# A transformer kernel of eight stages: z's convolution on the tensor engine in three chunks, rotated keys and queries by transfers in two, in another order

## The chip, the cores and the metric

The kernel runs on one core of a Trainium2 chip, in one launch. The core has five engines with a row of instructions each: PE (TensorE, matrix products into the eight banks of PSUM), DVE (VectorE), ACT (ScalarE), POOL (GpSimd) and SP (SyncE), which here issues the transfers. An engine takes its row strictly in order; engines wait for each other by semaphores. The metric is the device time of one execution in microseconds (us), median of several runs; less is better.

## The reference

Four layers, each an attention-like part and a feed-forward part, with a residual and a layer norm after each: eight stages, on 2048 tokens of width 128. The change touches two of them. Stage 0 is a state-space mixer:

```python
xz = jnp.einsum('bld,ed->ble', x, in_proj_w)
xs, zs = jnp.split(xz, 2, axis=-1)
xc = jax.nn.silu(_dwconv_same(jnp.swapaxes(xs, 1, 2), conv_x_w, conv_x_b))
zc = jax.nn.silu(_dwconv_same(jnp.swapaxes(zs, 1, 2), conv_z_w, conv_z_b))
# ... delta, B, C from xc; h = dA_t * h + dBu_t over 256 tokens, 64 x 16 states
y = jnp.concatenate([y, jnp.swapaxes(zc, 1, 2)], axis=-1)
return jnp.einsum('ble,de->bld', y, out_proj_w)
```

`_dwconv_same` is a convolution over four neighbouring tokens, each channel by itself. Stage 1 is an attention with 16 heads of width 8, of which 4 are plain and 4 are rotated by position, followed by a mixture of experts:

```python
k_rope = k_rope * cos + rotate_half(k_rope) * sin
q_rope = q_rope * cos + rotate_half(q_rope) * sin
kk = jnp.concatenate([k, k_rope], axis=-1)
qq = jnp.concatenate([q, q_rope], axis=-1)
```

`rotate_half` swaps the two halves of the four rotated dimensions; the signs are in the table of sines. Stages 2 to 7 are a linear attention, a feed-forward part with binarized weights, two more attentions and two more mixtures of experts.

## The kernel before

All data are fp32 and stay on the core. The tokens are cut into four chunks of 512 (two sequences of 256), and each chunk goes through the eight stages. Chunks 0 and 1 have a lane each; chunks 2 and 3 share the third: stages 0 to 3 of chunk 2, then of chunk 3, then stages 4 to 7 of both. Each lane has its part of one SBUF tile, `arena`; the weights lie in `W`, constants in `CF`, the residual in `X`, its transposition in `XT`.

A stage is a list of steps (`stage_steps`), each with parts on one engine after the other. `PARTS` says which: "P3.58 A.68" is a part of PE, then one of ACT, and the numbers are the planner's durations. The place of every part in its engine's row is written out in a table, `TURNS`, by step, stage and chunk; where a part may run on either of two engines (as "V.69|G1.28"), a minus sign chooses the second. `order_of_steps` sorts the parts by it and hands out PSUM banks. So the order of each engine's row is fixed by numbers.

The steps of which is spoken below:
- 0.n: layer norm and transposition (four 128x128 products on PE). 0.w: the four taps of the convolution times the projection's weights, on DVE.
- 0.in, number 0: projection and convolution of x, as four products of PE over shifted columns, then Silu on ACT. Number 1: the projection of z, one product; its convolution on DVE, a TENSOR_SCALAR (L1938) and three SCALAR_TENSOR_TENSOR (L1941); then Silu.
- 0.dt, 0.dr, 0.du, 0.bc: delta, its product with x, B and C. 0.wr and 0.rp: delta times x goes to HBM and comes back repeated over the states. 0.db: times B, on POOL (L2498). 0.da: delta repeated on PE, its exponential on ACT. 0.st: the scan over the tokens, on DVE (L2126), 16 per chunk. 0.hc: its state times C, on DVE (L1935) or POOL (L2502). 0.ac: the sum over states, on PE. 0.y to 0.e: output, residual, feed-forward and norms.
- 1.kq, number 0 for keys and 1 for queries: two products on PE, one with the weights and one with the weights of the swapped halves; DVE multiplies the first by cosines and the second by sines (L1935), POOL adds them (L2526). 1.km: keys masked by head, four copies. 1.sc, 1.ex, 1.nm, 1.tr, 1.pv: scores, exponential, normalization, transposition and product with the values.
- 3.p, numbers 0 and 1: stage 3's weights are binarized: a reduction (L2313) and other instructions of DVE, two of POOL and a transposition.
- 4.a, 4.g, 4.st, 4.l: weights of stage 4 multiplied ahead of time.
- The helpers: L1216 is every product of PE, L1220 every transposition, L1668 every ACT instruction, L1935 every TENSOR_TENSOR of DVE.

## Time and profile before

| | |
|---|---|
| runs | 1312.79, 1313.94 and 1316.95 us, median 1313.94 |
| profiled execution | 1316.18 us, its span 1314.2 us |
| mean granted clock of PE | 0.975 of full rate |
| PE busy | 1262.0 us, 96% |
| PE weight loads | 888.8 us, 68% (beside the products) |
| DVE busy | 927.8 us, 71% |
| ACT busy | 901.5 us, 69% |
| POOL busy | 777.6 us, 59% |
| transfers | 66.74 MB, 51 GB/s on average |

The span is the time from the first to the last instruction. Busy shares are averages over stages with different limits, so the profile is also read in stretches; a time in us below is counted from the span's start.
### The profile page before, as it was taken

What the parts mean: (1) busy time and instruction counts of PE and PEld (TensorE: products, weight loads), DVE (VectorE), ACT (ScalarE), POOL (GpSimd) and SP (SyncE); (2) the same over time, 40 slices, a digit from 0 to 9 for tenths busy, and PEclk for the clock granted to TensorE, in tenths of its full rate; (3) what the DMA queues carried; (4) which work ended last, traced back from release to release, by engine and by line L of the source; (5) the groups of instructions that cost most, each with busy time, mean ns of one, the idle gap of its engine ahead of it and who ended that gap; (6) DMA issues with size and microseconds to landing.
All of it is one profiled execution on the core that took longest, in us unless ns stands there. A gap on an engine that the chain in (4) does not pass through costs nothing.

```text
span 1314.2 us, 25939 instructions
## 1 busy us (share of the span) xinstructions
PE 1262.0 (96%) x8634; PEld 888.8 (68%) x8634; DVE 927.8 (71%) x3613; ACT 901.5 (69%) x2507; POOL 777.6 (59%) x853
## 2 busy tenths in 40 slices
PE   8799689999998999999999999999999999999997
PEld 4355356668744777777776777777788877776665
DVE  5979988867768788767656454787597678655254
ACT  6848899968574898766867666376778758765231
POOL 2989987668457867575655855356524524433434
PEclk9769989999998999999999999999999999999999
DMA  8753000110061000111000101101200011002430
GB/s 284 203 131 95 9 1 2 58 58 2 1 197 34 1 2 2 58 73 30 37 2 2 65 1 68 65 2 66 84 3 2 1 62 29 1 1 66 112 98 24
DMA packets 26373, 66.74 MB, mean 51 GB/s; under 512 B 2945, under 2 KB 7809, under 8 KB 25473
## 3 DMA queue, kind: packets, MB, share of 16 engines
q1 hardware_dynamic: 26240, 65.10, 16.4%
q8 instruction: 69, 1.13, 0.3%
q14 instruction: 64, 0.52, 0.1%
HBM read 61.74 MB, written 3.34 MB: 50 GB/s over the span
## 4 chain that ended last, share of the span: by engine, by line
PE 82%; DVE 9%; ACT 4%; POOL 2%; issue 2%; POOLq 0%; DVEq 0%; ACTq 0%
PE bank L1216 71%; PE bank L1220 11%; DVE arena L2126 2%; ACT arena L1668 2%; DVE arena L1935 2%; ACT L1668 1%; DVE stats L1949 1%; DVE arena L2192 1%; DVE stats L1938 1%; POOL arena L2566 1%; ACT bank L1668 1%; DVE arena L2190 1%; ACT X L1668 0%; POOL stats L2489 0%; DVE arena L2204 0%
## 5 line engine op out<-in xcount | busy, mean ns | idle before, releaser
L1668 ACT ACTIVATE arena<-arena 128x256 f32<-128x256 f32 (+4 forms) x804 | 355.6, 447 | 31.8 <-DVE arena L2192 15.0
L1668 ACT ACTIVATE arena<-bank 128x512 f32<-128x512 f32 (+3 forms) x354 | 190.9, 570 | 199.4 <-PE bank L1216 125.0
L1216 PE MATMUL bank<-XT,W 128*128 128x512 f32 (+1 forms) x720 | 287.5, 534 | 0.4 <-DVE arena L2204 0.3
L1216 PEld LDWEIGHTS bank<-W,arena 128*128 128x128 f32 x1888 | 230.2, 193 | 41.1 <-issue 35.7
L2513 POOL TENSOR_TENSOR arena<-arena 128x512 f32<-128x512 f32 (+2 forms) x108 | 171.3, 1600 | 137.5 <-DVE arena L1935 55.1
L1216 PE MATMUL bank<-W,arena 128*128 128x128 f32 (+1 forms) x1888 | 239.1, 277 | 1.1 <-POOL arena L2513 0.7
L1216 PE MATMUL bank<-arena 128*32 128x128 f32 (+8 forms) x2864 | 222.2, 335 | 6.9 <-DVE arena L2192 4.1
L2565 POOL TENSOR_TENSOR arena<-arena 128x256 f32<-128x256 f32 x192 | 118.6, 618 | 169.6 <-DVE arena L2198 169.1
L2566 POOL TENSOR_TENSOR arena<-arena 128x512 f32<-128x512 f32 x192 | 201.0, 1047 | 0.0
L1216 PEld LDWEIGHTS bank<-arena 128*32 128x32 f32 (+4 forms) x2864 | 147.0, 151 | 79.6 <-issue 52.8
L1220 PE MATMUL bank<-CF,arena 128*128 128x128 f32 x1312 | 181.7, 277 | 8.7 <-POOL arena L2566 5.3
L1216 PEld LDWEIGHTS bank<-XT,W 128*128 128x128 f32 x720 | 128.7, 192 | 84.5 <-issue 77.9
L1220 PEld LDWEIGHTS bank<-CF,arena 128*128 128x128 f32 x1312 | 150.2, 142 | 51.8 <-issue 38.9
L1216 PE MATMUL bank<-arena,W 128*128 128x512 f32 (+3 forms) x388 | 163.5, 663 | 15.3 <-DVE arena L2126 8.0
L1668 ACT ACTIVATION_READ_ACCUMULATOR arena<-arena 128x1 f32 x768 | 146.3, 190 | 0.0
L1668 ACT ACTIVATE arena<-bank,W 128x512 f32<-128x512 f32 (+1 forms) x180 | 103.0, 618 | 49.0 <-PE bank L1216 36.2
L2204 DVE COPY arena<-bank 128x512 f32<-128x512 f32 x147 | 98.1, 683 | 48.8 <-PE bank L1220 47.8
L1216 PEld LDWEIGHTS bank<-arena,W 128*128 128x128 f32 (+1 forms) x388 | 56.6, 200 | 85.3 <-issue 64.0
L1668 ACT ACT_TABLE_LOAD x82 | 105.2, 1283 | 11.2 <-DVE arena L1935 3.3
L1935 DVE TENSOR_TENSOR arena<-bank,arena 128x512 f32<-128x512 f32 x98 | 65.3, 684 | 67.3 <-PE bank L1216 57.4
L2192 DVE CUSTOM_DVE_ANT_0 arena<-bank,CB 128x256 f32<-128x256 f32 x256 | 107.3, 419 | 0.0
L2190 DVE CUSTOM_DVE_ANT_0 arena<-bank,CB 128x128 f32<-128x128 f32 x256 | 73.0, 285 | 30.9 <-PE bank L1216 29.2
(153 smaller groups left out, 1693.6 us busy)
## 6 DMA issues: line engine op xcount, KB each, us to landing
arena<-rws SPq DMA_DIRECT2D x44, 512.0 KB, 5.7
arena<-rep SPq DMA_DIRECT2D x62, 256.0 KB, 5.4
arena<-rws SPq DMA_DIRECT2D x8, 384.0 KB, 10.9
W<-w SPq DMA_DIRECT2D x1, 2692.0 KB, 9.1
...
```

The source lines that it names most:

```text
L1216: return e.matmul(o, lhsT, rhs, start=start, stop=stop, skip_group_check=True)
L1220: ins = e.transpose(bank[b.i][:, j * 128:j * 128 + s.shape[0]], s, cst("ident"))
L1668: return e.activation(o, a, func, **kw)
L1935: return e.tensor_tensor(o, a, b, op)
L1938: return e.tensor_scalar(o, a, s1_, s2_, op0, op1) if op1 is not None else e.tensor_scalar(o, a, s1_, None, op0)
L2126: e.tensor_tensor_scan(h, bank[a.i][:, :], h, 0.0, ALU.mult, ALU.add).then_inc(done[a.i], 1)
L2190: e.tensor_tensor_reduce(px[:, j * 384:j * 384 + 128], bank[b.i][:, 0:128], bias[:, 0:128], -1.0, 3.4e38, ALU.add, ALU.min, nm[:, 2 * j:2 ...
L2192: e.tensor_tensor_reduce(px[:, j * 384 + 128:(j + 1) * 384], bank[b.i][:, 128:384], bias[:, 128:384], -1.0, 3.4e38, ALU.add, ALU.min, nm[: ...
L2204: e.tensor_copy(third(s, c, n), bank[b.i][:, :]).then_inc(done[b.i], 1)
L2513: e.tensor_tensor(h, h, w, ALU.mult).then_inc(has["gw"], 1)
L2565: e.tensor_tensor(px[:, :, 0:128], px[:, :, 0:128], rec[:, :, 0:1].to_broadcast([128, 2, 128]), ALU.mult)
L2566: e.tensor_tensor(px[:, :, 128:384], px[:, :, 128:384], rec[:, :, 1:2].to_broadcast([128, 2, 256]), ALU.mult).then_inc(has["pn"], 1)
```

## The change

1. z's convolution. In chunks 0, 1 and 2 (all but `SHIFTED`) z is projected and convolved as x is, by four products of PE: step 0.in has a number 2, with the tap weights of z. The table of taps grows from 512 to 1024 columns, and 0.w with it. Chunk 3 keeps the old way.
2. The rotation. In chunks 1 and 3 (`MOVED`) 1.kq gives way to 1.rq: one product, copied to SBUF by ACT; SP moves the rows of the copy by eight small transfers to where the swapped half stands; DVE multiplies the moved copy by sines (in place, both operands in SBUF) and the bank by cosines; POOL adds. So that the swap is a shift of whole partitions, the 128 partitions of keys and queries are laid out by dimension within groups of four heads (`by_dim`), for all chunks; the scores are the same sums in another order.
3. The order. `TURNS` has other numbers throughout.

```diff
-    "0.in": ("P3.58 A.68", "P.87 V2.95 A.68"), "0.w": "V.6",
+    "0.in": ("P3.58 A.68", "P.87 V2.95 A.68", "P3.58 A.68"), "0.w": "V1.2",
+    "1.rq": "P.87 A.6 D2.6 V1.4 G1.27",
...
+MOVED = (1, 3)
+SHIFTED = (3,)
+def second_in(c):
+    return 1 if c in SHIFTED else 2
+def turned_by(c):
+    return "1.rq" if c in MOVED else "1.kq"
...
-        add("0.in", 1, ("0.bc", 0))
+        add("0.in", second_in(c), ("0.bc", 0), *([] if c in SHIFTED else [("0.w", 0, PREP)]))
...
-    ("0.n", 0, 0): (11, 13, 14, 18, 26), ("0.in", 0, 0): (29, 41, 93, 103, 117), ("0.dt", 0, 0): (44, 48, 55), ("0.dr", 0, 0):
```

On SP:

```diff
+                elif name == "1.rq":
+                    on.wait_ge(*after("kr", name, c, n))
+                    raw, to = s1(c, 3 + n), s1(c, 5 + n)
+                    for g in range(0, 128, 32):
+                        e.dma_start(to[g:g + 24, :], raw[g + 8:g + 32, :]).then_inc(d_kq[c][n], 16)
+                        e.dma_start(to[g + 24:g + 32, :], raw[g + 16:g + 24, :]).then_inc(d_kq[c][n], 16)
```

On PE:

```diff
-                    if n:
+                    if n == 1:
                         mm(ps[:, :], wt(0, "win")[:, 128:256], s0(c, 1)).then_inc(full[b.i], 1)
                         continue
...
-                        tap = wt(0, "tap")[:, k * 128:(k + 1) * 128]
+                        tap = wt(0, "tap")[:, k * 256 + 64 * n:k * 256 + 64 * n + 128]
...
+                elif name == "1.rq":
+                    b, ps = first(name, c, n)
...
+                    mm(ps[:, :], wt(1, "kq" if n else "kr"), s1(c, 1)).then_inc(full[b.i], 1)
```

On ACT:

```diff
+                        act(s0(c, 7 if n else 6), bank[b.i][:, :], ACT.Silu, bias=wt(0, "czb" if n else "cxb")).then_inc(done[b.i], 1)
...
+                elif name == "1.rq":
+                    b = u("b", name, c, n)
+                    on.wait_ge(*filled(b))
+                    act(s1(c, 3 + n), bank[b.i][:, :], ACT.Copy).then_inc(has["kr"], 1)
```

On DVE:

```diff
-                    tt(taps, taps, wt(0, "win")[:, 0:128].unsqueeze(1).to_broadcast([128, 4, 128]), ALU.mult).then_inc(has["taps"], 1)
+                    tt(taps, taps, wt(0, "win").unsqueeze(1).to_broadcast([128, 4, 256]), ALU.mult).then_inc(has["taps"], 1)
...
+                elif name == "1.rq":
...
+                    on.wait_ge(d_kq[c][n], 128)
+                    own(tt(tm, tm, sn, ALU.mult))
+                    tt(d, bank[b.i][:, :].rearrange("p (b l) -> p b l", b=2), cs, ALU.mult).then_inc(done[b.i], 1)
+                    on.wait_ge(*own.last())
```

On POOL:

```diff
+                elif name == "1.rq":
+                    d = s1(c, 3 + n)
+                    on.wait_ge(*emptied(u("b", name, c, n)))
+                    e.tensor_tensor(d, d, s1(c, 5 + n), ALU.add).then_inc(has["kq"], 1)
```

The layout of the partitions:

```diff
+def by_dim():
+    g, d, j = np.meshgrid(np.arange(4), np.arange(8), np.arange(4), indexing="ij")
+    return (32 * g + 8 * j + d).reshape(128)
```

How the rows move, at three places. The lines have other numbers after the change: L1216 becomes L1242, L1220 L1246, L1935 L1971, L1938 L1974, L1941 L1977, L2126 L2162. First, PE's row at the start, before: the convolution of x of chunk 2 (the third to fifth line), the transposition of chunk 0 (the first L1220), 0.dt of chunk 2, 0.bc of chunk 2 with a small product ahead, and the transposition of chunk 1.

```order
L1216 MATMUL bank<-arena,W 128x512
L1216 MATMUL bank<-arena,W 128x2x255 x2
L1216 MATMUL bank<-arena,W 128x2x254
L1216 MATMUL bank<-W 128x128
L1220 MATMUL bank<-CF,arena 128x128 x4
L1216 MATMUL bank<-arena,W 128x512
L1216 MATMUL bank<-W,CF 128x128
L1216 MATMUL bank<-arena,W 128x512 x2
L1220 MATMUL bank<-CF,arena 128x128 x4
L1216 MATMUL bank<-arena,W 128x512
L1216 MATMUL bank<-arena,W 128x2x255 x2
L1216 MATMUL bank<-arena,W 128x2x254
```

After:

```order
L1242 MATMUL bank<-arena,W 128x512
L1242 MATMUL bank<-arena,W 128x2x255 x2
L1242 MATMUL bank<-arena,W 128x2x254
L1246 MATMUL bank<-CF,arena 128x128 x8
L1242 MATMUL bank<-arena,W 128x512
L1242 MATMUL bank<-W,CF 128x128
L1242 MATMUL bank<-arena,W 128x512 x3
L1242 MATMUL bank<-arena,W 128x2x255 x2
L1242 MATMUL bank<-arena,W 128x2x254
L1242 MATMUL bank<-arena,W 128x512
L1242 MATMUL bank<-arena,W 128x2x255 x2
L1242 MATMUL bank<-arena,W 128x2x254
```

The transpositions of chunks 0 and 1 now stand together ahead of chunk 2's 0.dt, and behind the convolution of x of chunk 0 stands that of z of chunk 2.

Second, DVE's row at the first scans of chunk 2. Before, from the end of 0.du:

```order
L1935 TENSOR_TENSOR arena<-bank,arena 128x512
L1938 TENSOR_SCALAR arena<-bank,W 128x512
L1941 SCALAR_TENSOR_TENSOR arena<-bank,W,arena 128x2x255 x2
L1941 SCALAR_TENSOR_TENSOR arena<-bank,W,arena 128x2x254
L1935 TENSOR_TENSOR arena<-bank,arena 128x512
L2126 SCALAR_TENSOR_TENSOR arena<-bank,arena 128x512
```

After (the first row holds the end of 0.du and the input of the first scan):

```order
L1971 TENSOR_TENSOR arena<-bank,arena 128x512 x2
L2162 SCALAR_TENSOR_TENSOR arena<-bank,arena 128x512
L1971 TENSOR_TENSOR arena<-bank,arena 128x512
L2162 SCALAR_TENSOR_TENSOR arena<-bank,arena 128x512
L1974 TENSOR_SCALAR arena<-bank 128x512
```

The four instructions of z's convolution are gone from between; the second scan has moved ahead of chunk 0's 0.dt.

Third, DVE's row at the first rotations of stage 1 (`bank,CF` is a bank times cosines or sines). Before:

```order
L1935 TENSOR_TENSOR arena<-bank,CF 128x512 x2
L2126 SCALAR_TENSOR_TENSOR arena<-bank,arena 128x512
L2313 TENSOR_REDUCE pre<-W 128x4
L1938 TENSOR_SCALAR bw<-W 128x512
L1938 TENSOR_SCALAR pre<-pre 128x4
L1941 SCALAR_TENSOR_TENSOR bw<-W,bw 128x512
L1938 TENSOR_SCALAR bw<-bw,pre 128x128 x4
L1935 TENSOR_TENSOR arena<-bank,CF 128x512 x4
L2126 SCALAR_TENSOR_TENSOR arena<-bank,arena 128x512
```

After:

```order
L1971 TENSOR_TENSOR arena<-bank,CF 128x512 x2
L2162 SCALAR_TENSOR_TENSOR arena<-bank,arena 128x512
L1971 TENSOR_TENSOR arena<-arena,bank 128x512
L2162 SCALAR_TENSOR_TENSOR arena<-bank,arena 128x512
L1971 TENSOR_TENSOR arena<-arena,bank 128x512
L1971 TENSOR_TENSOR arena<-bank,CF 128x512 x4
L2162 SCALAR_TENSOR_TENSOR arena<-bank,arena 128x512
```

The five lines of 3.p are gone; two state products (0.hc) and a scan stand there. 3.p has moved behind the router of chunk 2, right ahead of chunk 1's first softmax.

## Rows read from the trace of the kernel before

**Rows 1.** The page: busy times, and the chain that ended last, by engine.

```profile
PE 1262.0 (96%) x8634; PEld 888.8 (68%) x8634; DVE 927.8 (71%) x3613; ACT 901.5 (69%) x2507; POOL 777.6 (59%) x853
...
PE 82%; DVE 9%; ACT 4%; POOL 2%; issue 2%; POOLq 0%; DVEq 0%; ACTq 0%
```

**Rows 2.** Busy time by stretch: length, busy (instructions) of each engine, clock, DMA.

```profile
0.00:225.00 225.00, 193.21 (x1256) 110.46 (x1257) 188.24 (x556) 175.65 (x433) 171.57 (x144) 0.88 0.36 106
...
30.00:54.00 24.00, 16.08 (x52) 5.37 (x50) 20.70 (x27) 21.67 (x30) 23.36 (x13) 0.79 0.72 186
...
92.00:118.00 26.00, 26.00 (x148) 14.53 (x147) 21.88 (x34) 18.87 (x28) 25.10 (x17) 1.00 0.55 142
...
118.00:153.00 35.00, 27.03 (x172) 15.13 (x170) 33.71 (x83) 27.26 (x61) 30.75 (x22) 1.00 0.13 38
...
153.00:225.00 72.00, 61.84 (x676) 43.36 (x677) 64.22 (x316) 68.63 (x259) 56.58 (x66) 0.93 0.01 2
...
225.00:345.00 120.00, 119.63 (x941) 84.26 (x940) 93.11 (x372) 94.63 (x266) 85.23 (x89) 1.00 0.10 32
...
345.00:420.00 75.00, 65.61 (x313) 38.16 (x312) 59.07 (x140) 45.44 (x71) 45.65 (x34) 0.95 0.36 101
...
420.00:1314.00 894.00, 883.54 (x6128) 655.89 (x6126) 587.33 (x2549) 585.77 (x1738) 475.13 (x586) 1.00 0.11 35
```

**Rows 3.** The same view, of the stretch at the lower clock.

```profile
54.00:82.00 28.00, 26.88 (x93) 12.66 (x94) 21.32 (x26) 16.09 (x23) 24.99 (x15) 0.51 0.54 150
```

**Rows 4.** PE's waits, first line: total, times, longest.

```profile
PE bank L1216 <- DVE arena L2126: 14.9, 9, 4.7
```

**Rows 5.** Timeline, PE at the start: start, duration, what, idle before.

```profile
9.50 3.58 PE L1216 MATMUL bank<-arena,W 128*128 128x512 f32 x8
...
13.49 0.66 PE L1220 MATMUL bank<-CF,arena 128*128 128x128 f32 x4
...
14.03 1.12 PE L1216 MATMUL bank<-arena,W 128*128 128x512 f32 x2
```

**Rows 6.** Timeline, DVE at the start; the weights' load, from the list of transfers.

```profile
7.51 0.69 DVE L1935 TENSOR_TENSOR W<-W 128x512 f32<-128x512 f32 x1
...
12.33 2.35 DVE L1938 TENSOR_SCALAR arena<-X,stats 128x128 f32<-128x128 f32 x8
...
24.28 0.75 DVE L1938 TENSOR_SCALAR arena<-bank,W 128x512 f32<-128x512 f32 x1 [1.23 <-PE bank L1216]
...
25.07 2.31 DVE L1941 SCALAR_TENSOR_TENSOR arena<-bank,W,arena 128x510 f32<-128x510 f32 x3
...
W<-w SPq DMA_DIRECT2D x1, 654.0 KB, 5.5
```

**Rows 7.** 0.hc: the line on POOL, and DVE's group of that shape.

```profile
L2502 POOL TENSOR_TENSOR arena<-arena x33: 1257/1271/1296, 29.8 to 155.2; 128x512 f32<-128x512 f32 x33
...
L1935 DVE TENSOR_TENSOR arena<-arena,bank 128x512 f32<-128x512 f32 x14 | 9.1, 668 | 0.0
```

**Rows 8.** Timeline at 3.p: DVE, then PE's wait, then POOL.

```profile
137.14 0.66 DVE L2313 TENSOR_REDUCE pre<-W 128x4 f32<-128x512 f32 x1
...
138.78 2.88 DVE L1938 TENSOR_SCALAR pre<-pre 128x4 f32<-128x4 f32 x1
...
143.46 2.47 DVE L1935 TENSOR_TENSOR arena<-bank,CF 128x512 f32<-128x512 f32 x4
...
144.88 1.52 PE L1216 MATMUL bank<-arena,W 128*128 128x512 f32 x3 [3.46 <-DVE arena L1935]
...
139.82 1.82 POOL L2548 MEMSET arena<- 128x2080 f32 x1
```

**Rows 9.** Small transfers of SP by line, and landing times of a 256 KB write.

```profile
L1172 SPq DMA_DIRECT2D rws<-arena x48: 269/290/345, 236.4 to 1265.6; - x48
...
L1159 SPq DMA_DIRECT2D rep<-arena x4: 320/332/432, 23.1 to 374.8; - x4
...
DMA to landing us min/median/max: 2.0/2.1/2.3
```

More of the change, by code:

```diff
@@ L286, in stage_steps @@
         add("1.vz", 0, ("1.r", 0))
-        add("1.kq", 0, ("1.n", 0), ("1.a", 0, PREP))
-        add("1.kq", 1, ("1.n", 0))
-        add("1.km", 0, ("1.kq", 0))
-        add("1.km", 1, ("1.kq", 0))
+        kq = turned_by(c)
+        add(kq, 0, ("1.n", 0), ("1.a", 0, PREP))
+        add(kq, 1, ("1.n", 0))
+        add("1.km", 0, (kq, 0))
+        add("1.km", 1, (kq, 0))
         add("1.v", 0, ("1.n", 0), ("1.a", 0, PREP), ("1.vz", 0))
-        attention(lambda u: [("1.kq", 1), ("1.km", 0), ("1.km", 1), ("1.v", 0)], lambda u: [])
+        attention(lambda u: [(kq, 1), ("1.km", 0), ("1.km", 1), ("1.v", 0)], lambda u: [])
         add("1.y", 0, *[("1.pv", u) for u in range(UNITS)])
@@ L360, in weight_steps @@
 def weight_steps():
-    loads = [("load", s, 0, [need for q in OVER[s] for c in range(NC) for need in ([("f", 0, c, q)] if q else [("0.in", 1, c, 0), ("0.dt", 0, c, 0)])]
+    loads = [("load", s, 0, [need for q in OVER[s] for c in range(NC) for need in ([("f", 0, c, q)] if q else [("0.in", second_in(c), c, 0), ("0.dt", 0, c, 0)])]
               + [("4.st", n, PREP, 0) for n in range(4) if s == 4]) for s in OVER]
@@ L820, in network @@
         d_wr = [sem(f"d_wr{c}") for c in range(NC)]
+        d_kq = {c: [sem(f"d_kq{c}_{n}") for n in range(2)] for c in MOVED}
         d_rp = [[sem(f"d_rp{lane}_{i}") for i in range(STATES // 2)] for lane in range(LANES)]
@@ L908, in decays0, with gated @@
             return uses["AB"[q % 2], "0.da", c, q - q % 2]
+        def gated(c):
+            return after("zc", "0.in", c, 1) if c in SHIFTED else emptied(u("b", "0.in", c, 2))
         def by_pe(c, q):
@@ L1140, in stage_over @@
                     else:
-                        on.wait_ge(*after("zc", "0.in", c, 1))
+                        on.wait_ge(*gated(c))
                         on.wait_ge(*filled(u("b", "0.dt", c)))
@@ L1323, in _ @@
                     on.wait_ge(*emptied(uses["Y", "0.ac", c, 0]))
-                    on.wait_ge(*after("zc", "0.in", c, 1))
+                    on.wait_ge(*gated(c))
                     for j in range(4):
@@ L1373, in _ @@
                     banks = [u(f"S{j}", name, c, n) for j in range(4)]
-                    on.wait_ge(*after("kq", "1.kq", c, 1))
+                    on.wait_ge(*after("kq", turned_by(c), c, 1))
                     on.wait_ge(*after("km_a", "1.km", c, 0))
@@ L1748, in _ @@
                         on.wait_ge(*filled(b))
-                        act(s0(c, 6), bank[b.i][:, :], ACT.Silu, bias=wt(0, "cxb")).then_inc(done[b.i], 1)
+                        act(s0(c, 7 if n else 6), bank[b.i][:, :], ACT.Silu, bias=wt(0, "czb" if n else "cxb")).then_inc(done[b.i], 1)
                 elif name == "0.bc":
@@ L1805, in _ @@
                 elif name == "1.km":
-                    on.wait_ge(*after("kq", "1.kq", c, 0))
+                    on.wait_ge(*after("kq", turned_by(c), c, 0))
                     for i in (n, n + 2):
@@ L2168, in _ @@
                 elif name == "1.km":
-                    on.wait_ge(*after("kq", "1.kq", c, 0))
+                    on.wait_ge(*after("kq", turned_by(c), c, 0))
                     for i in (n, n + 2):
@@ L2692, in constants @@
          "rows8": np.concatenate([(q[:, 0:32] == 8 * k + p % 8) for k in range(4)], 1).astype(np.float32),
-         "hm": (p // 8 % 4 == np.arange(4)[None, :]).astype(np.float32), "gm": (p % 32 < 8).astype(np.float32), "half": np.full((128, 1), np.float32(0.125))}
+         "hm": (p % 4 == np.arange(4)[None, :]).astype(np.float32), "gm": (p % 32 < 8).astype(np.float32), "half": np.full((128, 1), np.float32(0.125))}
     cf = np.concatenate([d[n] for n, _ in CONSTS], 1).astype(np.float32)
```

45 lines of the change are left out of this document (26 added, 19 removed), and 491 rows, old and new, of tables (EMITS, OPENS, PARTS, TURNS).

## The prediction

> **What bounds the kernel now.** I read the page first: PE is busy 96% of the span, DVE 71%, ACT 69%, POOL 59%, and the chain that ended last stands on PE for 82% of it [rows 1]. So PE work costs its own time wherever PE is full, and help for another engine pays only where PE waits. Where is that? The table by stretches tells [rows 2]: PE is busy 119.63 us of the 120 from 225 to 345, and 883.54 of the 894 after 420. Before 225 it is idle 225 - 193.21 = 31.8 us, and it loses more by its clock: the granted clock is at the lower of its levels (1.2 of 2.4 GHz) for nearly all of 54 to 82 [rows 3]. So the first 225 us are the one large place for a gain. From 345 to 420 it is busy 65.61 of 75; these 9.4 idle us lie in stage 0 of chunk 3, which the change leaves as it is.
>
> What holds PE there? The list of PE's waits has scans by DVE at its head, 14.9 us in 9 waits [rows 4]. But DVE isn't alone: between 30 and 54 POOL is busy 23.36 of 24, between 92 and 118 25.10 of 26, where PE is itself busy 26.00 of 26. After 153 ACT has 68.63 of 72 [rows 2]. DVE leads from 118 to 153: 33.71 of 35, PE 27.03. A microsecond taken from DVE is a microsecond gained only there and before the first scan.
>
> **z's convolution on PE, in chunks 0, 1 and 2.** Before, PE makes one product for z and DVE convolves it in four instructions. After, PE does the four shifted products that it does for x. A group of eight PE instructions (four products) took 3.58 us [rows 5], so one product is 0.89 and each chunk adds 2.7 us of PE, 8.1 in all. It frees DVE of 0.75 + 2.31 = 3.06 us per chunk [rows 6], 9.2 in all. ACT makes the same Silu, from another place.
> - Chunk 2. DVE's convolution begins at 24.28 and ends at 27.38, right ahead of the first scan's input [rows 6]: gain 3.06. The new products of PE stand where PE waits anyhow. But the start has two costs. The product over the taps doubles from 512 to 1024 columns, 0.69 to 1.38, and its load of 654 KB, landed 5.5 us after its issue, grows by 256 KB; in proportion that would be 2.2 us, of which I take 0.6, since some of the 5.5 is spent before data flow. The load of before had landed by 1.8 + 5.5 = 7.3, and DVE took it up at 7.51, so the product now ends at about 7.5 + 0.6 + 1.4 = 9.5, and the convolution of x, which began at 9.50, loses 0.2. Then PE's row: the transposition of chunk 1 now stands ahead of chunk 2's 0.dt. DVE's work for it was ready at 12.33 + 2.35 = 14.68; the longer product ahead of it takes what DVE had to spare there, so about 14.9, and the transposition takes 0.66: 0.dt starts at 15.6, not 14.03 [rows 5, 6]. That is 1.6 later, with the 0.2 in it. Sum: -3.1 + 1.6 = -1.5. Ends: -3.1 and +1.6, and 1.6 more if the load takes the whole 2.2.
> - Chunk 0. DVE is let off once more; PE's 2.7 us fit into what it is idle between 30 and 54, 24 - 16.08 = 7.9 [rows 2]. POOL is the engine that is full there, and the order moves 0.hc steps between the two: by counting them, DVE has 2 more in chunk 0, 2 more in chunk 1 and 1 fewer in chunk 2, so POOL is freed of 3 x 1.27 = 3.8 us and DVE gets 3 x 0.67 = 2.0 [rows 7]. I take -2.0 for the exchange, about half of what POOL gains, since PE at its lower clock holds both up between 54 and 92. Ends: -3.8 and +2.0.
> - Chunk 1. The row places its convolution around 100 us, where PE is full [rows 2]: +2.7. The ends are 0 and +5.4, at the lower clock.
>
> **3.p is moved.** The two binarizations of stage 3's weights are needed only by stage 3, and stood in DVE's row among the first rotations. The first took DVE from 137.14 to 143.46, 6.3 us, and PE waited 3.46 us for the rotation behind it [rows 8]. It now stands ahead of chunk 1's first softmax. I take -4.5, between that wait and the whole stretch; ends 0 and -6.3. The second has the same kinds of instruction and came after 153, where ACT is the busy one: I take -1.0, ends 0 and, at the first one's price, -6.3 [rows 2]. In the new place, from about 225, DVE is busy 93.11 of 120 us and PE full [rows 2]; the stretch stands before a softmax of chunk 1 alone. I take +1.0, ends 0 and +6.3.
>
> One instruction in [rows 8] deserves a look: a TENSOR_SCALAR on 128x4, the smallest work there, took 2.88 us. It ended at 141.66, with POOL's memset (139.82 + 1.82 = 141.64). The Trainium skill, "SBUF — State Buffer", section "Who interferes with whom", says why: VectorE in its two-port modes and GpSimd hold a shared port pair by turns, a whole instruction long, and also a VectorE instruction with two SBUF inputs contends with a GpSimd instruction that reads SBUF. The trace agrees for the first kind. The page speaks against the new rotation, whose product of two SBUF tiles is of the second kind: by the rule it could stand behind POOL as this one did, which the last rival below prices.
>
> **Rotated keys and queries by transfers (1.rq), chunks 1 and 3.** It drops one product per half, four in all: -0.89 x 4 = -3.5 us of PE, in stretches where PE is full [rows 2, 5]. ACT gains four copies, DVE has its two products of 0.67 as before, POOL its sum. What it adds is delay. A half passes: a copy on ACT, 0.6 by my estimate (a product's time of 0.67 on DVE [rows 7]), eight transfers issued by SP at 0.29 each 2.3, landing 2.1 after the last (2.0 to 2.3 for a write of 256 KB): 5.0 us where a second product of 0.89 stood, 4.1 later [rows 5, 9]. The second half of a chunk has the first one's eight issues ahead of it, 6.4 later. DVE takes its row in order, so if the transfers aren't there, it stands with softmaxes of other lanes behind it; a PSUM bank too is held through the transfer. The order places other work between: in chunk 1, counted by steps, the first product stands two steps behind the chunk's transposition in place of four, and DVE comes to it eight steps later than to the old rotation. I take 1.1 us per chunk, +2.2. Ends: 0, and all of 2 x 6.4 = 12.8.
>
> **The sum.** -1.5 - 2.0 + 2.7 - 4.5 - 1.0 + 1.0 - 3.5 + 2.2 = -6.6 us. The profiled execution took 1316.18 us (span 1314.2), the median of the runs is 1313.94, 2.2 below it; the change is taken from the median: 1307.3 us.
>
> **The rivals.**
> - The clock. More products before 54 us leave PE less idle, and the stretch at the lower level from there may shrink or go. PE was busy 26.88 of 28 there; at the higher rate it would need half, but POOL needs 24.99 of the 28, so that at most 3.0 us come free: 1304.3 [rows 3]. For it: PE is sparse, 16.08 of 24, just ahead of that stretch, and the change puts 2.7 us there. Against: the start is late by 1.6. The Trainium skill, "TensorE: Matmul & The Clock Gate", section "What's actually happening", says that the rate follows how busy PE has been; by that rule this rival would hold, and the trace agrees in so far as the long low stretch follows a sparse one.
> - Relief that reaches nobody. POOL holds 30 to 118 and ACT what follows 153 [rows 2]; then the gains at the start, of the exchange and of 3.p (1.5, 2.0, 4.5 and 1.0) fall away, and 2.7 + 1.0 - 3.5 + 2.2 = +2.4 is left: 1316.3. For it: the busy shares. Against: PE's wait of 3.46 us for DVE, right behind 3.p.
> - Late transfers, the slower case. Chunk 1 comes to its rotation when the two other lanes are at the end of their attention and DVE is busy about nine tenths; if DVE stands for the landing in both chunks, the whole 12.8 us are paid in place of 2.2: -6.6 + 10.6 = +4.0, 1317.9. The new product of two SBUF tiles may besides stand behind a POOL instruction of 1.27 us each time, as the TENSOR_SCALAR did behind the memset [rows 7, 8]: 4 x 1.27 = 5.1, and alone it would make 1312.4. It decides from the point where DVE waits at 1.rq for more than 2.2 + 6.6 = 8.8 us in all. Against it: one chunk has two other lanes beside it each time, and PE is full after 420.
> - The change does what it says in any case: the products and transfers are in the rows of the new order.
>
> **From cases to numbers.** About 0.3% of 1314, 3.9 us, is what a measurement of this kernel can tell from no change. Forecast 0.48, own range 1303.3 to 1311.3; clock 0.17; no relief 0.22; late transfers 0.13. Of the forecast 0.07 lies within 3.9 us, so faster is 0.41 + 0.17 = 0.58. Within: 0.07 of the forecast, 0.15 of "no relief", 0.03 of the late transfers, 0.25. Slower: 0.07 + 0.10 = 0.17. The range runs to 1298.5 below, since the start and 3.p may both give their full price beside the clock, and to 1318.5 above.
>
> **What would show it.** First scan of DVE before 27.5 us; 0.dt of chunk 2 at about 15.6; three PE groups of eight more before 120; the first scores of stage 1, which follow on the rotation that PE waited for at 144.88, some 5 us earlier; PE's idle time before 225 down from 31.8 by those 5 and the 8.1 us of new products, 13 in all; DVE's wait for the transfers under 3 us in all; busy PE +4.6 us at equal clock. The forecast is wrong if that first rotation reaches PE no earlier than 144, or if DVE waits at 1.rq for over 8 us, or if a new wait appears ahead of chunk 1's softmax.

## The result, and the profile after

The changed kernel takes 1337.54 us (median of 4 runs, 1332.68 to 1341.45), the kernel before beside it 1314.49 us. The ratio is 1.0165, 95% interval 1.0143 to 1.0187: slower by 23 us, where 6.6 us less was forecast. Its profiled execution took 1341.45 us, its span 1339.7 us. It is the longest of the four, which lie in two pairs, near 1333 and near 1341 us. One run of e1 below took 1622.14 us at a granted clock of 0.743, and is left out of e1's ratio.

The page after: busy times, the clock in 40 slices, and the chain that ended last, by engine and by line.

```profile
PE 1277.2 (95%) x8644; PEld 898.1 (67%) x8644; DVE 920.3 (69%) x3608; ACT 901.4 (67%) x2507; POOL 771.6 (58%) x849
...
PEclk9769999899998979999999999999999999999999
...
PE 78%; DVE 8%; ACT 5%; POOL 3%; issue 2%; SPq 2%; DMA 1%; POOLq 0%; DVEq 0%; ACTq 0%
PE bank L1242 68%; PE bank L1246 10%; ACT arena L1700 4%; DVE arena L2162 2%; DVE arena L1971 1%; POOL arena L2543 1%; SPq L1184 1%; DVE arena L2237 1%; DVE stats L1985 1%; POOL arena L2547 1%; DVE stats L1974 1%; ACT L1700 1%; SPq L1185 1%; DVE arena L2235 1%; ACT X L1700 1%
```

Against [rows 1]: PE's share of the chain fell from 82% to 78%, and two newcomers stand in it, "SPq" (SP issuing transfers) and "DMA". L1184 and L1185 are the two `dma_start` lines of `1.rq`. 3% of 1340 us are 40 us: small shares of a chain are no small change.

Busy time by stretch, as in [rows 2, 3], and the two places that will matter (225 to 250 and 464 to 493):

```profile
0.00:225.00 225.00, 197.28 (x1256) 111.58 (x1257) 171.87 (x531) 170.21 (x424) 160.97 (x137) 0.89 0.36 107
225.00:250.00 25.00, 18.27 (x132) 10.59 (x130) 16.32 (x70) 17.36 (x52) 12.78 (x14) 0.86 0.20 50
...
440.00:464.00 24.00, 23.43 (x142) 17.55 (x140) 18.68 (x76) 19.92 (x47) 16.54 (x21) 1.00 0.00 1
464.00:493.00 29.00, 20.99 (x119) 16.02 (x119) 15.91 (x64) 16.66 (x58) 14.89 (x18) 0.71 0.08 19
...
30.00:54.00 24.00, 20.26 (x51) 7.41 (x52) 17.27 (x22) 15.77 (x24) 17.25 (x11) 0.72 0.72 184
54.00:82.00 28.00, 21.80 (x84) 8.30 (x82) 20.54 (x25) 16.24 (x22) 28.00 (x17) 0.72 0.48 133
...
118.00:153.00 35.00, 34.24 (x180) 21.62 (x177) 30.66 (x65) 27.87 (x54) 30.88 (x22) 0.90 0.16 46
153.00:225.00 72.00, 60.55 (x702) 40.43 (x701) 65.68 (x333) 69.95 (x269) 55.40 (x66) 1.00 0.01 2
225.00:345.00 120.00, 113.06 (x892) 80.22 (x890) 93.63 (x366) 93.81 (x268) 87.22 (x90) 0.97 0.12 37
```

By the first 225 us little is lost: the same 1256 matmuls as in [rows 2], PE idle for 27.7 us in place of 31.8. The stretch from 225 on, where PE had been full, isn't full any more.

**Where the lag grows.** Shares don't tell when time was lost. Both programs run the same steps (the order's names), so I took for each step of PE its start after less its start before, and the median over the steps that began in a stretch of 20 us of the kernel before. The columns to the right are the experiments' profiled executions, told below; plus is later, in us.

| stretch of before | after | e1 no transfers | h1 also old order late | i4 h1 with transfers | e7 | b1 3.p alone | f2 z alone |
|---|---|---|---|---|---|---|---|
| 120 | 9.9 | 3.7 | 4.1 | 4.5 | 10.1 | -0.3 | 3.7 |
| 200 | 0.9 | -5.5 | -5.0 | -4.6 | 1.3 | -3.5 | 2.2 |
| 220 | 1.9 | -2.7 | -2.8 | -3.6 | 2.2 | -3.5 | 2.2 |
| 240 | 8.8 | -0.6 | -1.8 | 4.0 | 7.8 | -1.9 | 2.2 |
| 260 | 9.8 | 0.4 | -0.8 | 4.9 | 8.8 | 0.7 | 2.2 |
| 340 | 9.0 | -0.5 | -1.1 | 4.7 | 7.9 | 2.1 | 2.2 |
| 380 | 12.4 | 4.4 | 1.6 | 6.2 | 9.8 | 3.1 | 3.5 |
| 440 | 12.7 | 5.1 | 0.8 | 4.8 | 6.3 | 3.2 | 4.1 |
| 460 | 25.9 | 11.4 | 0.8 | 20.9 | 19.5 | 3.2 | 4.1 |
| 1240 | 24.9 | 10.5 | 0.7 | 20.8 | 18.4 | 3.1 | 4.0 |

The column "after" has two jumps: 7 us at 240 and 13 at 460. Nothing happens after 480. The 10 us of lag at 120 are nearly gone at 200, where ACT is the busy one. Single executions differ: b1 and i2, below, hold the same instructions in their first 130 us and are 4.3 us apart at 120 (-0.3 and -4.6). So a difference of 3 or 4 us in one column is not a finding; the jumps are. They stand in e2's execution too, 7.3 us at 240 and 13.2 at 460, in a program that differs from the changed kernel in z's convolution alone.

**The first jump.** The chain of waits from 225 to 255, by line, and its pieces (start, length, what):

```profile
by line: PE bank L1242 26.4%; SPq L1184 20.1%; SPq L1185 14.8%; issue 7.4%; DMA arena<-arena 6.5%; DVE arena L2237 4.6%; PE bank L1246 3.4%; ACT arena L1700 3.3%; DVE arena L2235 3.1%; DVE arena L1971 3.1%; DVE arena L2039 2.1%; PE bank L14
...
225.80 0.88 SPq L1184
...
232.19 0.75 SPq L1184
...
237.31 1.97 DMA arena<-arena
239.33 0.57 issue
239.91 0.68 DVE arena L1971
```

SP's sixteen issues for chunk 1's queries and keys stand end to end from 225.80 to 237.93, 12.1 us, 0.76 each with the gaps. The second half's eight begin only at 232.19. What DVE did meanwhile:

```profile
231.13 0.68 DVE L1971 TENSOR_TENSOR arena<-arena,X 128x512 f32<-128x512 f32 x1
233.72 0.69 DVE L1971 TENSOR_TENSOR arena<-arena,CF 128x512 f32<-128x512 f32 x1 [1.91 <-DMA arena<-arena]
...
234.93 0.18 DVE L1971 TENSOR_TENSOR arena<-bank,W 128x32 f32<-128x32 f32 x1
239.30 0.69 DVE L1971 TENSOR_TENSOR arena<-arena,CF 128x512 f32<-128x512 f32 x1 [4.19 <-DMA arena<-arena]
239.91 0.68 DVE L1971 TENSOR_TENSOR arena<-bank,CF 128x512 f32<-128x512 f32 x1
240.51 0.17 DVE L1974 TENSOR_SCALAR arena<-arena 128x32 f32<-128x32 f32 x1
```

The rows on 128x32 are the router of chunk 2 (`1.rt`): the first part done at 235.1, the second queued behind chunk 1's keys until 240.5. PE, in both places (timeline):

```profile
236.89 1.04 PE L1246 MATMUL bank<-CF,arena 128*128 128x128 f32 x8
243.30 0.45 PE L1494 MATMUL bank<-CF,arena 128*128 128x128 f32 x1 [5.38 <-DVE arena L1977]
...
469.27 1.98 PE L1242 MATMUL bank<-XT,W 128*128 128x512 f32 x4
474.75 1.28 PE L1242 MATMUL bank<-W,arena 128*128 128x128 f32 x8 [3.50 <-DVE arena L1971]
...
481.05 8.93 PE L1242 MATMUL bank<-arena 128*128 128x65 f32 x56 [4.17 <-DVE arena L1971]
```

L1494 is `1.wt`, the transposition of the router's shares: PE waits 5.38 us for another chunk's router. At 464 to 493, chunk 3's rotation, PE waits 3.50 and 4.17 us, and the table of stretches has a granted clock of 0.71 there, PE busy 20.99 of 29 us, and of 1.00 in the stretch ahead, PE busy 23.43 of 24: PE had idled, and the level fell. DVE's waits by cause, and PE's, over the whole span:

```profile
DVE arena L1971 <- DMA arena<-arena: 13.2, 4, 4.2
```

```profile
PE bank L1242 <- DVE arena L1971: 11.3, 5, 4.2
...
PE bank L1494 <- DVE arena L1977: 5.5, 2, 5.4
```

### The profile page after: what moved, and what is told of

Read it like the earlier page. It is cut to its first block, busy times and chain, and to the rows that moved or that the text cites. A ratio compares the mean times of both kernels' runs of the same rounds, so it can differ in the third digit from the quotient of the medians.

```text
span 1339.7 us, 25973 instructions
## 1 busy us (share of the span) xinstructions
PE 1277.2 (95%) x8644; PEld 898.1 (67%) x8644; DVE 920.3 (69%) x3608; ACT 901.4 (67%) x2507; POOL 771.6 (58%) x849
## 4 chain that ended last, share of the span: by engine, by line
PE 78%; DVE 8%; ACT 5%; POOL 3%; issue 2%; SPq 2%; DMA 1%; POOLq 0%; DVEq 0%; ACTq 0%
PE bank L1242 68%; PE bank L1246 10%; ACT arena L1700 4%; DVE arena L2162 2%; DVE arena L1971 1%; POOL arena L2543 1%; SPq L1184 1%; DVE arena L2237 1%; DVE stats L1985 1%; POOL arena L2547 1%; DVE stats L1974 1%; ACT L1700 1%; SPq L1185 1%; DVE arena L2235 1%; ACT X L1700 1%
## 5 line engine op out<-in xcount | busy, mean ns | idle before, releaser
L1242 PE MATMUL bank<-XT,W 128*128 128x512 f32 (+1 forms) x720 | 288.6, 534 | 0.4 <-DVE arena L1971 0.2
L1242 PEld LDWEIGHTS bank<-W,arena 128*128 128x128 f32 x1888 | 232.6, 195 | 43.9 <-issue 33.0
L1242 PE MATMUL bank<-W,arena 128*128 128x128 f32 (+1 forms) x1888 | 242.8, 279 | 4.6 <-DVE arena L1971 3.5
L1242 PE MATMUL bank<-arena 128*32 128x128 f32 (+8 forms) x2864 | 223.8, 336 | 11.6 <-DVE arena L1971 4.2
L1242 PEld LDWEIGHTS bank<-arena 128*32 128x32 f32 (+4 forms) x2864 | 149.8, 152 | 85.8 <-issue 55.9
L1246 PE MATMUL bank<-CF,arena 128*128 128x128 f32 x1312 | 179.8, 277 | 11.0 <-POOL arena L2615 6.2
L1246 PEld LDWEIGHTS bank<-CF,arena 128*128 128x128 f32 x1312 | 149.5, 142 | 52.3 <-issue 42.6
L1242 PEld LDWEIGHTS bank<-XT,W 128*128 128x128 f32 x720 | 128.3, 191 | 83.7 <-issue 77.2
L1242 PE MATMUL bank<-arena,W 128*128 128x512 f32 (+3 forms) x398 | 170.7, 664 | 13.8 <-DVE arena L2162 9.7
L1242 PEld LDWEIGHTS bank<-arena,W 128*128 128x128 f32 (+1 forms) x398 | 60.0, 202 | 88.4 <-issue 75.0
L1971 DVE TENSOR_TENSOR arena<-bank,arena 128x512 f32<-128x512 f32 x98 | 65.4, 684 | 71.5 <-PE bank L1242 55.8
```

The source lines that it names most:

```text
L1242: return e.matmul(o, lhsT, rhs, start=start, stop=stop, skip_group_check=True)
L1246: ins = e.transpose(bank[b.i][:, j * 128:j * 128 + s.shape[0]], s, cst("ident"))
L1971: return e.tensor_tensor(o, a, b, op)
```

## The experiments

Each stands beside runs of the kernel before; numbers in the diffs of the order's table are places in the order.

**e1, the second product again.**

```diff
-MOVED = (1, 3)
+MOVED = ()
-("1.rq", 1, 1): (680, 689, 692, 708, 713, 670, 675, 681, 702, 707)
+("1.kq", 1, 1): (680, 692.5, 713, 670, 681.5, 707)
-("1.rq", 1, 3): (1416, 1420, 1426, 1443, 1446, 1419, 1424, 1438, 1449, 1453)
+("1.kq", 1, 3): (1416, 1426.5, 1446, 1419, 1438.5, 1453)
```

> The changed kernel, with the rotated keys and queries of chunks 1 and 3 by a second product on PE again, and DVE's two products at the place where the transfers would begin; all else (z's convolution, 3.p's place, the order) stays. Theory T (the transfers' issue: 16 transfers take SP 12.1 us in a row, 225.80 to 237.93, DVE stands 13.2 us in four waits and the lag against the kernel before grows from 1 to 9 us at chunk 1 and from 13 to 26 us at chunk 3): the lag stays at about 1 us through the router of chunk 2 and at 2 to 4 us after 500, 1315 to 1320 us. Rival R (the start: PE's added convolutions at the lower clock level and the later chunks): the transfers stand where there was slack, and 1330 us or more stay. Rival C (the new order as a whole, with 30 us more at the lower clock level): 1328 to 1338 us.

1327.04 us, ratio 1.0079 [1.0049, 1.0109]. Half of the loss goes with the transfers, more than rival R allows; but theory T wanted 1315 to 1320, and the time is 1 us below rival C's range. The table shows what is left: no lag from 140 to 340, then 4 us at 380, 5 at 440 and 11 at 460, with no transfer of rotated rows in the program. So there is a second cause, in no theory as I had put them: perhaps the order, but of what runs behind 340 us, and not as a whole, as rival C has it. h1 puts that to the test.

**e2, z by DVE again.**

```diff
-SHIFTED = (3,)
+SHIFTED = (0, 1, 2, 3)
```

> The changed kernel, with z's convolution by one PE product and four DVE instructions in all four chunks again; transfers, 3.p's place and the order stay. Theory T: PE's start is faster up to 130 us, but ACT-bound work from 153 to 225 takes the lead back as it did the lag (8.5 us at 115, 0.65 at 207), so 1333 to 1341 us. Rival R: the lag of 6 to 10 us before 150 goes and stays away, 1312 to 1322 us. Rival C: 1328 to 1341 us.

1337.51 us, ratio 1.0168 [1.0137, 1.0200], the changed kernel's own 1.0165. Rival R falls: within this order z's convolution has no part in the loss that these times can tell, and its 1312 to 1322 us are far off. The two profiled executions end 7 us apart (a lag of 17.9 us here, 24.9 after), though the medians are equal: this one was the shortest of its four, the other the longest. So an execution's end counts for less than the times.

**e6, half of the transfers.**

```diff
-MOVED = (1, 3)
+MOVED = {(1, 1), (3, 0)}     # (chunk, half): queries of 1, keys of 3
```

> The changed kernel with only one half of each chunk by transfers: chunk 1's queries and chunk 3's keys; the other half by a second PE product. Half of SP's issues, 8 in a row, and nothing queued ahead of them. Theory T: DVE's first wait (1.9 us in chunk 1, 3.7 us in chunk 3) stays, the second (4.2 and 3.4) is gone, PE's wait of 5.4 us for the router's shares too: 1320 to 1330 us. Rival R: 1335 us or more. Rival C: 1328 to 1341 us, with no relation to the number of transfers.

1326.61 us, 1.0085 [1.0059, 1.0111]: the same as e1. One half by transfers costs nothing that the times can tell; the transfers' 11 us come with the second. DVE has no wait for a transfer in chunk 1, where theory T left one of 1.9 us, and one of 0.96 us in chunk 3, where it left 3.7. SP's issues in chunk 1 and DVE's product, as two views, and the wait in chunk 3:

```profile
221.45 0.88 SPq L1184 DMA_DIRECT2D arena<-arena  x1
...
227.20 0.63 SPq L1185 DMA_DIRECT2D arena<-arena  x1
```

```profile
228.72 0.68 DVE L1971 TENSOR_TENSOR arena<-arena,X 128x512 f32<-128x512 f32 x1
229.32 0.69 DVE L1971 TENSOR_TENSOR arena<-arena,CF 128x512 f32<-128x512 f32 x1
...
459.79 0.69 DVE L1971 TENSOR_TENSOR arena<-arena,CF 128x512 f32<-128x512 f32 x1 [0.96 <-DMA arena<-arena]
```

The last issue ends at 227.83, and 1.5 us later DVE multiplies, without a wait. So the order had room for eight issues and a landing, in chunk 3 all but 1 us of it, not for sixteen.

**e4, half of the issues on ACT.**

```diff
 # SP, 1.rq
-    e.dma_start(to[g + 24:g + 32, :], raw[g + 16:g + 24, :]).then_inc(d_kq[c][n], 16)
 # ACT, 1.rq, behind its copy
+    for g in range(0, 128, 32):
+        e.dma_start(to[g + 24:g + 32, :], raw[g + 16:g + 24, :]).then_inc(d_kq[c][n], 16)
```

> The changed kernel with the 8-partition half of the transfers issued by ACT in place of SP (four per half, right behind its copy), the 24-partition ones by SP as before. SP's row falls from 16 issues to 8, some 6 us, and the last one is issued by 232 in place of 237.93; ACT pays 4 issues per half. Theory T (the issue sets the wait): DVE's waits fall from 13.2 us to 5 us or less, and the time to 1322 to 1333 us, with ACT's own issues, 2.5 to 3 us a half, as what is lost. Rival L (a landing of 1.5 to 2.5 us and the distance to the product are what counts, not the issues): waits and time stay, 1336 to 1341 us.

1333.88 us, 1.0137 [1.0116, 1.0159], 3.7 us under the changed kernel and 0.9 above theory T's range; the two intervals overlap. Of DVE's 13.2 us of waiting for transfers one wait of 1.2 us is left, in chunk 3; rival L falls by the waits, and by the time as well, if narrowly. But ACT's rows show who pays:

```profile
223.26 3.33 ACTq L1836 DMA_DIRECT2D arena<-arena  x4
226.69 0.60 ACT L1699 ACTIVATE arena<-bank 128x512 f32<-128x512 f32 x1 [3.46 <-issue]
...
229.54 2.67 ACTq L1836 DMA_DIRECT2D arena<-arena  x4
232.26 1.28 ACT L1699 ACTIVATE arena<-arena,stats 128x128 f32<-128x128 f32 x4 [2.75 <-issue]
```

Four issues hold ACT for 3.33 and 2.67 us, twice per chunk, and PE's first wait from 225 to 520 is now one for ACT, 12.5 us in 5 times. An issue is paid by whoever makes it.

**e7, the keys' products behind the router.**

```diff
-("1.rq", 1, 1): (680, 689, 692, 708,   713,   670, ...)
+("1.rq", 1, 1): (680, 689, 692, 712.5, 713.5, 670, ...)
```

> The changed kernel, transfers and all; only DVE's two products for chunk 1's keys stand behind the router's shares of chunk 2 and no longer ahead of them. Theory T (DVE stands in order for the transfers, and who pays is what is queued behind): PE's wait of 5.4 us for those shares goes, DVE's of 4.2 us falls under 2, the lag at 240 us falls from 8.8 to 3 to 5: 1328 to 1335 us. Rival S (the keys themselves are what PE needs, so the first scores of chunk 1 are late by the same amount): 1335 to 1341 us.

1332.95 us, 1.0121 [1.0096, 1.0145]: 4.6 us come back. From 200 to 260 DVE waits for transfers, and PE for L1494:

```profile
DVE arena L1971 <- DMA arena<-arena: 2.7, 2, 1.8
```

```profile
PE bank L1494 <- DVE arena L1977: 1.1, 1, 1.1
```

Both waits shrink as theory T said (from 6.1 and 5.4 us). Yet the lag at 240 is 7.8, not 3 to 5: from 225 to 345 PE now waits 2.6 us for DVE's products (L1971), 0.9 after the change, which is rival S's side of it. Only 1 us of lag is gone by 340. The rest appears behind 360, most of it at 420, where the lag is 6.2 in place of 12.7, and there the two programs have the same order. The stretch from 420 to 430, of the changed kernel and of e7:

```profile
420.00:430.00 10.00, 6.97 (x24) 2.38 (x24) 9.97 (x11) 2.32 (x5) 8.81 (x8) 0.72 0.00 0
```

```profile
420.00:430.00 10.00, 6.96 (x37) 3.18 (x37) 9.69 (x12) 4.01 (x9) 7.87 (x7) 1.00 0.00 0
```

PE is busy for the same time, at 0.72 and at 1.00. So most of what e7's execution gains comes with the clock's level there, and whether the place of the keys' products has to do with that, one execution of each doesn't tell. Each theory held in part.

**h1, the old order behind 335 us.** e1, with the old order's numbers for every step behind about 335 us, of all chunks (284 rows of the table).

> The changed kernel without its transfers (the rotation's second product on PE, as in the first experiment), and for every step that stands behind about 335 us in both orders the order of the kernel before. Theory O (beside the transfers the new order of chunk 3 costs: step by step that first experiment was 0.5 us ahead of the kernel before at 340 us, 4.4 behind at 380 and 11.3 behind at 460): these 11 us go, 1311 to 1318 us. Rival K (the loss there is the clock's, or is owed to what stands ahead of 335 us): 1323 to 1329 us, as without this edit.

1316.96 us, 1.0011 [0.9994, 1.0028]: level with the kernel before. Theory O is shown: beside the transfers, it was the new order behind 335 us that cost. The edit takes back all of that order; that chunk 3 is the place is read from the table, where e1's lag grows between 340 and 480 alone, while chunk 3 passes its stages 0 and 1. In the rest of the document "the new order of chunk 3" stands for this. In e1, from 465:

```profile
465.00:470.00 5.00, 2.71 (x31) 2.39 (x33) 2.30 (x7) 3.86 (x10) 5.00 (x7) 1.00 0.00 0
470.00:475.00 5.00, 5.00 (x41) 3.90 (x37) 3.27 (x23) 4.31 (x18) 1.04 (x2) 0.62 0.02 7
```

PE is busy 2.71 of 5 us, and the stretch behind is granted 0.62. Which of the moved steps makes PE wait there wasn't tried.

**i4, the transfers put into h1.** The control: h1 with `1.rq` in both chunks, in chunk 1 where the changed kernel has it, in chunk 3 at the old product's places.

> The changed kernel with its transfers, and the order of the kernel before for what stands behind 335 us; chunk 3's products stand where they stood before, with two steps between product and DVE in place of eight. Theory T+O (the lag of 9 us at 260 is the transfers' of chunk 1; in chunk 3 the old order has no room for them, so that DVE stands for two times 8 issues and landings, 8 and 5 us): lag 8 to 9 at 340, 20 to 25 after 470, 1334 to 1341 us. Rival O (in chunk 3 the order made for the transfers cost all of it): 1323 to 1328 us.

1338.97 us, 1.0169 [1.0145, 1.0194]; the transfers and their places are all that sets it apart from h1, 21 us by the two ratios, each taken against its own runs of the kernel before (20 by the two profiles). The same stretches of h1, then of i4:

```profile
450.00:470.00 20.00, 19.59 (x151) 14.84 (x151) 17.74 (x82) 18.89 (x63) 16.53 (x22) 1.00 0.01 2
470.00:490.00 20.00, 19.80 (x188) 15.01 (x187) 16.00 (x69) 18.78 (x63) 12.93 (x19) 1.00 0.01 2
```

```profile
450.00:470.00 20.00, 14.43 (x88) 10.01 (x84) 10.41 (x34) 13.12 (x45) 12.30 (x12) 0.87 0.10 23
470.00:490.00 20.00, 15.67 (x89) 13.27 (x90) 11.29 (x57) 9.70 (x32) 9.32 (x14) 0.53 0.02 5
```

PE loses 9.3 us of work to idleness there, and the clock falls to 0.53 behind it: 177 matmuls in the 40 us in place of 339. DVE stands 16.5 us for transfers in i4, 10.4 of them in chunk 3, where the changed kernel has 7.1. Against h1's column the lag grows by 6.7 us from 220 to 340 and by 16.1 from 440 to 460. With e1 this says what the new order of chunk 3 does: it gives the transfers room. It costs some 9 us; without it the transfers cost 21 us in place of 11, so that the two come out level. Theory T+O holds by the time and by the lag of 20.9 at the end; at 340 the lag is 4.7, not 8 to 9. Rival O falls.

**b1, 3.p alone moved.**

```diff
-("3.p", 3, PREP): (393, 426, 435, 445, 457, 480, 499, 507)
+("3.p", 3, PREP): (734.25, 748.26, 785.27, 798.28, 810.29, 847.3, 854.31, 858.32)
```

> The kernel before with nothing changed but 3.p: the two binarizations of stage 3's weights stand ahead of chunk 1's first softmax, as in the changed kernel. Theory O: the first rotations come 4 to 6 us earlier, and DVE repays it at the new place, where PE is full and waits for the first scores behind 3.8 us of it: 1312 to 1318 us, no change. Rival P (the prediction's own step): the gain of 4.5 us and 1.0 stays, less 1.0: 1307 to 1311 us.

1319.21 us, 1.0020 [1.0004, 1.0035]. The column shows both halves: 3.6 us gained at 140 (-0.3 to -3.8), 1.6 lost at the first new place, 4.1 at the second. The time is above both ranges: 1312 to 1318 of theory O, which has the course right and the second place's price too low, and 1307 to 1311 of rival P. At the second new place DVE's row has, ahead of chunk 0's router:

```profile
257.38 0.68 DVE L2313 TENSOR_REDUCE pre<-W 128x1 f32<-128x512 f32 x1
```

**f2, z alone on PE.** The old order, with PE's four products for z in chunks 0 to 2.

> The kernel before with nothing changed but z's convolution, by PE in chunks 0, 1 and 2 as in the changed kernel, each at its old place. Theory O: the delays of PE's row before 130 us are taken up by the waits for ACT from 153 to 225, 1313 to 1318 us. Rival R (PE's added products at the lower clock level cost 5 to 6 us a piece): 1319 to 1326 us.

1324.07 us, 1.0068 [1.0040, 1.0097], from 1318.51 to 1333.71. The time lies in rival R's range and above theory O's: in the old order z on PE costs, where e2 found nothing in the new one. The profiled execution, near the low end (span 1318.2), has a lag of 6.1 at 40 us and 2.2 from 200 on; what made the longer ones longer wasn't profiled, and stays open.

**i2, i3 and i1: is there a better one?** b1, h1, and h1 with z on DVE, each with the second half of 3.p moved on to about 270 us:

```diff
-("3.p", 3, PREP): (..., 810.29, 847.3, 854.31, 858.32)
+("3.p", 3, PREP): (..., 861.5, 884.5, 905.5, 908.5)
```

> The kernel before with 3.p moved, its first half ahead of chunk 1's first softmax and its second half to about 275 us. With the second half ahead of chunk 0's router the lead of 1.9 us at 256 us became a lag of 2.1. If the place decides: 1312 to 1315 us, 2 to 4 us under that run. Rival (the moved work costs its own 4 us wherever PE is full): 1317 to 1320 us.

1313.32 us, 0.9975 [0.9960, 0.9989], 12 runs against 23 of the kernel before: the one version that beats both, and within the 1312 to 1315 expected. The gain is a quarter of a per cent, and its profile can't say from where: its lead of 4.4 us at the end it already had at 120 us (4.6), ahead of the first changed instruction, when its granted clock from 54 to 82 was 0.74, not 0.51 [rows 3]:

```profile
54.00:82.00 28.00, 25.47 (x124) 13.03 (x124) 24.99 (x40) 15.59 (x22) 27.30 (x17) 0.74 0.55 149
```

Within it, 3.p gains 3.6 us at 140 and gives 3.6 back by 280. Against b1's timing it is 0.45% better by the two ratios, which agrees with the place of the second half deciding; the same edit in h1 (i3) gained nothing, so that isn't shown. The gain against before rests on the interval alone.

> The kernel of the run with the old order late (1317), with z's convolution still on PE, and the second half of 3.p at about 275 us. If the place decides: 1313 to 1316 us. Rival (it costs its own time wherever PE is full): 1316 to 1319 us.

1320.22 us, 1.0026 [1.0011, 1.0040]: no gain from the same edit in h1, whose interval overlaps. The expected 1313 to 1316 was wrong, and the rival's 1316 to 1319 is 1 us too low.

> The kernel of the run with the old order late (no transfers, 3.p moved), with z's convolution by DVE again in all chunks, and the second binarization of 3.p moved on from the place ahead of chunk 0's router (257 us) to one behind a chunk 1 step near 275 us, where DVE waited 2.5 us for PE in the kernel before. If the places of 3.p cost as measured (3.8 us gained before 220, 1.9 us of it left at 256, 4 us lost at the second one), half of these 4 us come back, and z's return gives up to 4 us more: 1307 to 1313 us. Rival: whatever is gained before 340 is taken up by the wait at chunk 3's start and by the clock: 1313 to 1318 us.

1325.89 us, 1.0060 [1.0036, 1.0084]: above both ranges, and worse than i3 by 5.7 us. Here z back on DVE costs, as z on PE did in the old order (f2); but e2, the same edit beside the transfers, cost nothing. That z's edit costs wherever the order was made for the other is a guess that fits i1 and f2 and not e2. What is shown is that gains measured in another order didn't add.

## Why the prediction was wrong

The runs split the change in three, each by a difference of ratios and each with some 3 to 5 us either way:

| part | terms of the sum | forecast | measured |
|---|---|---|---|
| start and 3.p (h1) | -1.5 - 2.0 + 2.7 - 4.5 - 1.0 + 1.0 | -5.3 | +1.5 |
| order behind 335 us (e1 less h1) | none | 0 | +9 |
| rotation by transfers (after less e1) | -3.5 + 2.2 | -1.3 | +11 |

Together they are 22 us, the ratio 1.0165 (23 us between the two medians).

**The step that failed** is the wait for the transfers, "+2.2. Ends: 0, and all of 2 x 6.4 = 12.8", which cost some 14.5 us (below), and in it the price of an issue: "eight transfers issued by SP at 0.29 each 2.3". 0.29 is [rows 9]'s time for transfers of 8 partitions and 128 columns, from SBUF to HBM. The new ones go from SBUF to SBUF, with 512 columns on 24 and on 8 partitions, and took 0.73 and 0.62. Their size alone isn't the reason: the other line of [rows 9], a write of 128 partitions by 512 to HBM, took 0.33. The trace of before had a nearer row, transfers that end in the same SBUF tile, SP's issues of `0.rp`:

```profile
25.14 5.11 SPq L1166 DMA_DIRECT2D arena<-rep  x8
```

0.64 each. With it a half takes 5.1 and both 10.2 us of SP alone (measured: 6.3 and 12.1 with the gaps). The order's distance of eight steps, which I took as cover, had room for one half: e6 shows that, and the second half is what costs. "The second half of a chunk has the first one's eight issues ahead of it, 6.4 later" was the right thought at half its size: at its prices both halves and the landing make 2.3 + 2.3 + 2.1 = 6.7 us, and 13.5 were measured from SP's first issue to the second product at 239.30. The Trainium skill, "DMA: Bandwidth & Descriptors", section "Anatomy of one DMA — SWDGE (gpsimd) path", which tells of transfers issued from POOL, puts the fixed cost of some 2 us mostly into the completion and gives the sequencer's dispatch about 50 ns. For SP's it doesn't carry over: the last transfer landed 1.97 us after its issue began, near those 2 us, but a single issue held SP for 0.62 to 0.88 us; in a row of sixteen the issues decide and the landing is paid once. (The sum set the 2.1 us behind the last issue; in [rows 9] they count from its start, so it was 0.3 too long there.)

**The bound from above failed too.** I ended the term at DVE's whole wait, 12.8 us, and DVE stood 13.2 us, so as a wait the bound was nearly right. As a cost it was too low. The changed kernel less e1 is 11 us, and the transfers spare PE 3.5 us of products besides, so that the waits cost some 14.5, an estimate from the two; in the old order of chunk 3 DVE stood 16.5 us, and i4 less h1 is 21 us, with the same 3.5 spared. Two things can stand between. The wait stops whatever is queued behind, here another chunk's router, for which PE then waited 5.4 us (e7 takes that away, and by its profile it returns 1 us by 340). And PE's idle time comes with the lower clock: 0.71 in the 29 us at 464, 0.53 in i4. How the 21 us divide between waiting and clock wasn't separated. The Trainium skill, "TensorE: Matmul & The Clock Gate", section "What's actually happening", has the rate follow how busy PE has been; the stretches of e1, i4 and the changed kernel agree. I had used that rule for a gain only, at the start, and never for a loss behind a new wait. The range's other end, 1298.5, follows from no sum: 1304.3 less the full prices of the start (1.6) and of 3.p's first half (1.8) is 1300.9, with its second half's 5.3 as well 1295.6.

**The rival was right in kind.** "Late transfers" named place and mechanism, had a chance of 0.13, and put the time at 1317.9, 19.6 us too low. Its other half, products of two SBUF tiles standing behind POOL, did not occur: the four took 0.69 us each, and POOL, which waits for them, was idle beside all four, so no run here shows what the Trainium skill says of such products in "SBUF — State Buffer", section "Who interferes with whom".

**The order was never priced.** I compared counts of steps and looked at three places; the new order of chunk 3 wasn't one of them: of its stage 0 I had written "which the change leaves as it is". e1 against h1 makes it 0.68%, 9 us, next to the transfers the largest part of the miss.

**3.p.** "-4.5" for the first half: b1 gained 3.6. After the change too the lag falls by 3.9 there (9.9 at 120, 6.0 at 140); the rotation itself, 144.88 before, starts at 152.54, since the whole row was late by then. "-1.0" for the second: nothing seen. "+1.0" in the new place: 1.6 and 4.1. I had said that it stands before a softmax of chunk 1 alone; the second half stands ahead of chunk 0's router. In sum +2.6 by time in place of -4.5.

**z's convolution.** The rows of after at the start (PE, DVE, POOL):

```profile
15.03 1.02 PE L1242 MATMUL bank<-arena,W 128*128 128x512 f32 x2
...
39.66 9.17 PE L1242 MATMUL bank<-arena,W 128*128 128x512 f32 x17
...
28.59 0.69 DVE L1971 TENSOR_TENSOR arena<-bank,arena 128x512 f32<-128x512 f32 x1 [4.35 <-PE bank L1242]
29.32 1.22 DVE L2162 TENSOR_TENSOR_SCAN arena<-bank,arena 128x512 f32<-128x512 f32 x1
...
52.13 1.27 POOL L2547 TENSOR_TENSOR arena<-arena 128x512 f32<-128x512 f32 x1 [6.07 <-DVE arena L2162]
```

Chunk 2: 0.dt was said to start at 15.6, and started at 15.03; the first scan was said to come before 27.5, and came at 29.32. z's products did not stand where PE waits anyhow: they stand ahead of `0.da` in PE's row, and the scan's input waited 4.35 us for PE; before, this scan began at 28.46. Chunk 1: the four products ran from 108.61 to 112.30, 3.7 us in place of 1.1, the forecast's +2.7. Chunk 0: "PE's 2.7 us fit into what it is idle"; they ran from 42.66 to 47.77 within the long PE row, 5.1 us, largely at the lower level, and POOL, said to be the full engine, stood idle 6.07 us at 52.13. This rests on one execution, and the 10 us that it adds up to at 120 shrink to 0.9 by 200: "relief that reaches nobody" holds for losses as well, and that rival's 153 to 225 with ACT at 68.63 of 72 [rows 2] was rightly read.

**The exchange of 0.hc**, -2.0, can't be told apart in these runs. **The clock's rival** had its premise: the stretch from 54 to 82 was granted 0.72 in place of 0.51. But there PE was busy 21.80 us in place of 26.88 and POOL 28.00 of 28: nothing came of it.

**Idle time of PE before 225** is 225 - 197.28 = 27.7 us, said to be 31.8 - 13 = 18.8. Busy PE is up by 15.2 us, not 4.6. The other 10.6 fit the clock, whose mean fell from 0.975 to 0.967: 0.8% of 1277 us is 10.5.
